# Attention weights transposed and multiplied for pairs of head groups; raw-row transposes between the down-projections

## The reference, cut to what matters

```python
x = x + xattn(layernorm(x), ctx)
    # q, k, v projections; scores = q k^T / sqrt(32)
    # out = softmax(scores) @ v            per head, 77 keys
    # h = relu(out @ W1 + b1); h @ W2 + b2
x = x + ffn(layernorm(x))
    # top1 = argmax(xn @ Wg.T); y = expert[top1](layernorm(xn))
```

## Time and profile before

| | us |
|---|---|
| median of three runs | 1548.53 (1547.26 to 1549.6) |
| the profiled execution | 1549.81 |
| its span, first to last instruction | 1548.0 |
| PE busy | 1503.9 |
| DVE busy | 1005.6 |
| ACT busy | 711.5 |
| POOL busy | 428.8 |

### The profile page before, as it was taken

The page is one execution under the profiler, slowest core; times in us unless marked ns, Lnnn a source line. Parts: engine busy times, 40 slices in busy tenths (PEclk is TensorE's granted clock), DMA queues, the critical chain, the costliest instruction groups (busy, mean ns, idle before and its releaser), DMA issues.

```text
span 1548.0 us, 24311 instructions
## 1 busy us (share of the span) xinstructions
PE 1503.9 (97%) x7988; PEld 1257.0 (81%) x7988; DVE 1005.6 (65%) x2489; ACT 711.5 (46%) x2015; POOL 428.8 (28%) x312
## 2 busy tenths in 40 slices
PE   7689999999999999999999999999999999999998
PEld 4578888888888787878788888888887878778986
DVE  5735656575857576666757585757574756559666
ACT  3534535354536363545445353535363635424554
POOL 2512212222222222212122112222222222117776
PEclk9799999999999999999999999999999999999999
DMA  9310110213020202131211201030202011458883
GB/s 231 113 55 28 31 53 7 76 26 108 13 89 28 89 28 75 36 97 42 75 42 40 78 15 61 16 110 1 82 1 83 1 55 55 171 172 282 243 238 120
DMA packets 76951, 122.71 MB, mean 79 GB/s; under 512 B 27990, under 2 KB 36455, under 8 KB 75806
## 3 DMA queue, kind: packets, MB, share of 16 engines
q1 hardware_dynamic: 66030, 87.47, 19.6%
q0 software_dynamic: 10800, 33.70, 5.7%
HBM read 76.24 MB, written 46.72 MB: 79 GB/s over the span
## 4 chain that ended last, share of the span: by engine, by line
PE 78%; DVE 14%; ACT 4%; issue 2%; DMA 1%; POOL 1%; POOLq 0%; DVEq 0%; SPq 0%; ACTq 0%
PE bank L1034 23%; PE bank L1056 20%; PE bank L896 11%; PE bank L920 5%; PE bank L1014 5%; DVE actH L1003 4%; PE bank L1457 4%; PE bank L1501 3%; ACT actH L997 2%; PE bank L1125 2%; PE bank L1440 2%; PE bank L864 2%; DVE E L941 1%; DVE mx L929 1%; DVE sm L968 1%
## 5 line engine op out<-in xcount | busy, mean ns | idle before, releaser
L1056 PE MATMUL bank<-w,actH 128*128 128x512 f32 x1536 | 371.1, 392 | 0.0
L1034 PE MATMUL bank<-actA,w 128*128 128x512 f32 x1536 | 366.8, 394 | 0.0
L1034 PEld LDWEIGHTS bank<-actA,w 128*128 128x128 f32 x1536 | 286.0, 188 | 62.3
L1056 PEld LDWEIGHTS bank<-w,actH 128*128 128x128 f32 x1536 | 283.1, 188 | 54.9
L979 POOL TENSOR_TENSOR E<-E,rc 128x1232 f32<-128x1232 f32 x64 | 145.0, 2266 | 464.6 <-DVE rc L974 464.6
L1041 ACT ACTIVATE actH<-bank,b 128x512 fp32r<-128x512 f32 x128 | 88.2, 689 | 228.8 <-PE bank L1034 228.8
L1046 DVE TENSOR_TENSOR actH<-bank,actH 128x512 fp32r<-128x512 f32 x128 | 87.8, 686 | 159.6 <-ACT bank L1042 159.6
L896 PE MATMUL bank<-actA,wq 128*128 128x512 f32 x768 | 182.0, 390 | 0.0
L952 ACT ACTIVATE E<-bank,mx 128x77 f32<-128x77 f32 x512 | 157.8, 364 | 42.1 <-DVE mx L929 42.1
L896 PEld LDWEIGHTS bank<-actA,wq 128*128 128x128 f32 x768 | 144.1, 188 | 30.4 <-issue 0.5
L1199 POOL DMA_INDIRECT region<-rows,pos x64 | 62.3, 974 | 373.2 <-DVE pos L1193 334.0
(11 more groups left out here) (166 smaller groups left out, 1970.2 us busy)
## 6 DMA issues: line engine op xcount, KB each, us to landing
rowB<-region SPq DMA_DIRECT2D x71, 258.0 KB, 3.8
xn<-in_x SPq DMA_DIRECT2D x64, 256.0 KB, 2.8
rows<-in_x SPq DMA_DIRECT2D x64, 256.0 KB, 3.2
e_raw<-in_E SPq DMA_DIRECT2D x16, 256.0 KB, 2.8
region<-padrow SPq DMA_DIRECT2D x9, 258.0 KB, 3.9
w_raw<-in_W SPq DMA_DIRECT2D x1, 2048.0 KB, 11.8
w_raw<-in_W SPq DMA_DIRECT2D x2, 1024.0 KB, 8.7
e_parts<-e_high SPq DMA_DIRECT2D x8, 256.0 KB, 2.0
```

The lines of the kernel that those rows point to most:

```text
L1034: mm = pe.matmul(p[:], w, a, start=k == 0 and j == 0, stop=k == KD - 1 and j == 2)
L1056: mm = pe.matmul(p[:], a, w, start=m == 0 and j == 0, stop=m == MF - 1 and j == 2)
```

## The change

- `PT` and `AV` run for two pairs of groups. A pair has 616 keys, cut into chunks of 128, 128, 128, 128 and 104. The third chunk holds keys of both groups. `AV` is three steps: i = 0 (chunks 0, 1), i = 1 (chunk 2), i = 2 (chunks 3, 4), each in a bank of its own. ACT copies the bank of i = 1 to `csb`, and DVE adds its last 32 rows to those of i = 0 and its first 32 to those of i = 2; only then both are copied and subtracted into `actA`.
- `TT` for tiles 0 to 2 stands in the score phase, behind the steps of groups 1 to 3; tile 3 and `L`, `LT` stand among `PT` and `AV`. The transposed rows go to `actA` instead of `actQ`, the logits to `csb`.
- The one-hot is a step of its own (`OH`) behind the subtraction of H2. The row statistics (`X2STAT`) begin to drip behind H0.
- H0 and H1 run their first three k-steps together, then the last one of each.
- `vbd` has pairs, and its loads are 24 pieces a batch instead of 12.

```diff
-CH = [103, 103, 102]
+CH = [128, 128, 128, 128, 104]
+CA, CC, CB = (0, 1), (2,), (3, 4)
...
         def attention_tail(b):
-            for c in range(NC):
-                step("PT", b, 0, c)
+            step("PT", b, 0, 0)
+            step("PT", b, 0, 1)
             step("SUM", b, KD - 1)
             if b:
-                step("X2STAT", b - 1)
-            for g in range(KD):
-                if g + 1 < KD:
-                    for c in range(NC):
-                        step("PT", b, g + 1, c)
-                if b and g == KD - 2:
-                    for s in range(SUB):
-                        step("TT", b - 1, s)
-                step("AV", b, g)
+                step("TT", b - 1, SUB - 1)
+            for c in range(2, NC):
+                step("PT", b, 0, c)
+            if b:
+                step("L", b - 1)
+            step("AV", b, 0, 0)
+            if b:
+                step("LT", b - 1)
+            step("AV", b, 0, 1)
+            step("PT", b, 1, 0)
+            step("AV", b, 0, 2)
+            for c in range(1, 4):
+                step("PT", b, 1, c)
+            step("AV", b, 1, 0)
+            step("PT", b, 1, 4)
+            step("AV", b, 1, 1)
+            step("AV", b, 1, 2)
...
+            if b:
+                step("X2STAT", b - 1)
             for m in range(MF):
...
-                if not (b and m == 2):
-                    step("HLO", b, m)
-                if b and m == 0:
-                    step("L", b - 1)
+                step("HLO", b, m)
...
                 if b and m == 2:
-                    step("LT", b - 1)
-                    step("HLO", b, m)
+                    step("OH", b - 1)
...
                     if g + 2 < KD:
                         step("Q", b + 1, g + 2)
+                    if g >= 1:
+                        step("TT", b, g - 1)
...
+        def dve_av(dve, b, pr, i):
+            n = NP * b + pr
+            if i == 0:
+                return
+            if i == 1:
+                dve.wait_ge(S["act_c"], n + 1)
+                dve_add(dve, b, pr, 0)
+                return
+            dve.wait_ge(S["pe_av"], 3 * n + 3)
+            dve_add(dve, b, pr, 2)
+            for h in (0, 2):
+                g = 2 * pr + h // 2
+                dve.wait_ge(S["act_o"], KD * b + g + 1)
+                dve.tensor_tensor(actA[:, 1, g, :], of("AV", b, pr, h)[:], f32(actA[:, 0, g, :]), ALU.subtract
+                                  ).then_inc(S["dve_o"], 1)
+
+        def dve_add(dve, b, pr, i):
+            p, r = of("AV", b, pr, i), PART[i]
+            dve.tensor_tensor(p[r, :], p[r, :], csb[r, :], ALU.add).then_inc(S["dve_c"], 1)
...
         def pe_h(pe, b, m):
+            if m == 0:
+                own_bank(pe, "H", b, 1)
+                for k in range(KD - 1):
+                    pe.wait_ge(S["dve_o"], KD * b + k + 1)
+                    h_products(pe, b, 0, k)
+                for k in range(KD - 1):
+                    h_products(pe, b, 1, k)
+                pe.wait_ge(S["dve_o"], KD * b + KD)
+            for k in range(KD - 1 if m < 2 else 0, KD):
+                mm = h_products(pe, b, m, k)
             mm.then_inc(S["pe_h"], 1)
```

More of the change, by code:

```diff
@@ L1004, in dve_pt, with pe_av @@
                               f32(actH[0:CH[c], 0, j % SLOTS, :]), ALU.subtract).then_inc(S["dve_pt"], 1)
-        def pe_av(pe, b, g):
-            p = own_bank(pe, "AV", b, g)
-            pe.wait_ge(ld_v, 16 * VLOADS * (b // BPB + 1))
-            for c in range(NC):
-                j = NC * g + c
-                pe.wait_ge(S["dve_pt"], NC * KD * b + j + 1)
-                for i, (v, w) in enumerate(split3([vbd[0:CH[c], h, g, c, :] for h in range(2)],
+        def pe_av(pe, b, pr, i):
+            p = own_bank(pe, "AV", b, pr, i)
+            if pr == 0 and i == 0:
+                pe.wait_ge(ld_v, 16 * VLOADS * (b // BPB + 1))
+            mine = (CA, CC, CB)[i]
+            for c in mine:
+                j = NC * pr + c
+                pe.wait_ge(S["dve_pt"], NC * NP * b + j + 1)
+                for t, (v, w) in enumerate(split3([vbd[0:CH[c], h, pr, c, :] for h in range(2)],
@@ L1013, in pe_av @@
                                                   [actH[0:CH[c], h, j % SLOTS, :] for h in range(2)])):
-                    mm = pe.matmul(p[:], v, w, start=c == 0 and i == 0, stop=c == NC - 1 and i == 2)
+                    mm = pe.matmul(p[:], v, w, start=c == mine[0] and t == 0, stop=c == mine[-1] and t == 2)
             mm.then_inc(S["pe_av"], 1)
-        def act_av(act, b, g):
-            act.wait_ge(S["pe_av"], KD * b + g + 1)
-            act.activation(actA[:, 0, g, :], of("AV", b, g)[:], ACT.Identity).then_inc(S["act_o"], 1)
@@ L1026, in pe_h @@
+        def dve_add(dve, b, pr, i):
+            p, r = of("AV", b, pr, i), PART[i]
+            dve.tensor_tensor(p[r, :], p[r, :], csb[r, :], ALU.add).then_inc(S["dve_c"], 1)
         def pe_h(pe, b, m):
-            p = own_bank(pe, "H", b, m)
+            if m != 1:
+                own_bank(pe, "H", b, m)
             if b == 0:
                 pe.wait_ge(S["pool_w1"], 2)
-            for k in range(KD):
-                pe.wait_ge(S["dve_o"], KD * b + k + 1)
-                for j, (w, a) in enumerate(split3([w1[:, h, k, P * m:P * m + P] for h in range(2)],
-                                                  [actA[:, h, k, :] for h in range(2)])):
-                    mm = pe.matmul(p[:], w, a, start=k == 0 and j == 0, stop=k == KD - 1 and j == 2)
@@ L1037, in act_h, with h_products @@
+        def h_products(pe, b, m, k):
+            p = of("H", b, m)
+            for j, (w, a) in enumerate(split3([w1[:, h, k, P * m:P * m + P] for h in range(2)],
+                                              [actA[:, h, k, :] for h in range(2)])):
+                mm = pe.matmul(p[:], w, a, start=k == 0 and j == 0, stop=k == KD - 1 and j == 2)
+            return mm
         def act_h(act, b, m):
@@ L1096, in x2T @@
         def x2T(b):
-            return x2T_last if b == NBLK - 1 else actQ
+            return x2T_last if b == NBLK - 1 else actA
         def pe_tt(pe, b, s):
```

116 lines of the change are left out of this document (66 added, 50 removed).

## The result

| | before | changed |
|---|---|---|
| median of the timed runs | 1547.89 us (1546.12 to 1549.6) | **1700.1 us** (1698.49 to 1703.81) |
| profiled execution | 1549.81 | 1703.81 |
| its span | 1548.0 | 1701.9 |
| PE busy | 1503.9 | 1525.6 |

A forecast was written before the change was run, and what follows sets the result against it. PE, busy 97% of the span, bounds the kernel. To 1549.8 us the walk added 15 x (3.65 + 0.2 + 1.6) + 8 x 4.6 - 1 = 118, removed work deducted, giving 1668; the clock's 32 made 1700, range 1625 to 1745.

The forecast's parts named there:

- Removed work: PE's 6 matmuls and 8 transposes fewer a block: 2.2 us a block, 35 us in all, if nothing waits.
- A: PE's wait at the second chunk transpose for DVE's addition of the last row tile: 2.4 us, 15 times.
- B: PE's wait at the gate product for DVE's subtraction of raw tile 3: 3.3 us, 15 times.
- C: PE's waits at AV of the second pair: 1.0 us in two parts, 0.2 more at the last chunk, 15 blocks.
- E: PE's wait at the e_acc product after H1, in eight blocks preparing expert weights: 4.6 us, bounds 3.4 and 5.2.
- F: PE's wait for the one-hot after H3, at its first matmul: 1.6 us in 15 blocks, bounds 0.5 and 2.1.
- `vbd` loads: Doubled loads on SP's queue in three blocks delay xn loads: 0, at worst 4 us in the block preparing no weights.
- The clock: Low PE clock after idle waits: 12 us behind E, 20 behind A and B in half of the blocks; 32 together.
- rival 1: PE's clock stays up despite the waits, so the time is 1668; chance 0.25.
- rival 2: The clock falls in every tail and at every E wait, costing 3 us each: about 1725; chance 0.15.
- rival 3: Only the waits in H are real; ACT and DVE have room to hide the tail: 1580; chance 0.1.
- rival 4: Faster: DVE runs far enough ahead that PE's removed work is the whole effect, 1515; chance 0.03.

The follow-up runs named there:

- e11: e7 with the vbd loads moved behind the loads of the next block's rows and of the raw expert weights; 1522.8 us (0.9832).
- e3: Changed kernel with raw-row tile 1 transposed after the scores of group 3 instead of behind those of group 2; 1667.5 us (1.0749).
- e4: Changed kernel with the sum of the fourth group behind raw tile 3 and the last chunk of pair 0; 1663.6 us (1.0731).
- e1: Changed kernel with the e_acc sums issued on DVE ahead of H0's subtraction; 1658.0 us (1.069).
- e2: Changed kernel with the rank products behind H4 instead of H3; 1688.65 us (1.0894).
- e5: Changed kernel with the four edits of e1, e2, e3 and e4 together; 1569.6 us (1.0136).
- e6: Changed kernel with extra transposes, results overwritten, on PE during its waits at the gate product (24) and the e_acc product (38); 1679.7 us (1.0848).
- e7: Changed kernel with e1's and e2's edits, raw tiles, sum, gate product and pair 1 transposes reordered, H0 and H1 sharing two k-steps first; 1540.8 us (0.9954).
- e12: Changed kernel with the edits of e1 and e2 together; 1648.8 us (1.0635).
- e9: Changed kernel with only the vbd loads moved behind the token loads of the next block; 1704.6 us (1.0989).
- e10: Changed kernel with only the pairs of groups, merge and vbd kept; raw rows, gate, one-hot, statistics and H0, H1 as before the change; 1595.8 us (1.0296).

## Why the prediction was right, step by step

- **Removed work**, 2.2 us a block: 2.6 by e11. The twelve transposes of 128 columns take 1.47, those of 103 took 1.48, so width cost nothing. My other reason was weak: the 158 ns of the earlier trace rows is a mean over two shapes, 172 for 103 columns and 132 for 102, so it says little about width. The changed kernel's weight loads take 149 for 128 columns and 146 for 104. The rule of the Trainium skill that I had set against it ("TensorE: Matmul & The Clock Gate", "Step-by-step: what each phase is for") does not show in the time here.
- **A**, 2.4: 2.02 idle, 2.21 from start to start (from the start of the transposes ahead of it to the next start, less 0.103 a transpose; the idle time of a trace begins after the last transpose has drained). Cause shown by e3.
- **B**, 3.3: 2.83, or 3.06 from start to start. Cause shown by e4: a later sum takes 1.6 off it.
- **C**, 1.2 with its second part: 0.76. H0's wait of 0.2: its 24 matmuls take 5.95 for 5.5.
- **E**, 4.6: 4.12. From H0's start to the product it is 10.07, less 5.52 of matmuls 4.55, where the walk had 4.8 with H0's wait. Cause shown by e1.
- **F**, 1.6 (its own terms add up to 1.5): 1.3. e2 took it away.
- **`vbd` loads**, 0 with 4 as the worst: 2.7 in the block that prepares no weights (91.9 against 89.2). Inside the bound of 4, and so small only because E covers the loads in the other two blocks (e1).
- **The walk as a whole.** A block that prepares no weights takes 89.17 for 82.0, less 1.56 of clock 5.6; the walk had 5.45. The others take 95.4 for 82.48, less some 3.0 of clock 9.9; the walk had 10.05. Of the 152 us of the loss some 118 are left without the clock, and the walk had 118.
- **The clock**, 32: 34.2, but not for the reasons given. I had E at 12: eight falls of 2.7, less 9.6 because F would shrink. It is 16.3: a fall costs 2.0 on average there, and F does not shrink (1.3 in each of 14 blocks). I had the tail fall in half of the blocks at 2.7 each, 20; it falls in all 15, is paid in 12, and costs 1.5 there, 17.9. The Trainium skill's rule on bursts and waits (the same page, "HAM oscillation — how this bites in real kernels") holds for the changed kernel in that every tail falls; the tails of e5, with waits of 1.1 us and less, have no fall. Priced at 2.7 each it gave 20 us too much, since a part of the low clock falls into a wait.

So rival 1 (the clock stays up) is refuted by e6 and by the granted clock. Rival 2 is refuted in its price though not in its count, rival 3 (the tail is hidden) and rival 4 by the waits A and B. What made the forecast hold was the walk through three queues; from start to start its waits A, B and E are 5 to 10% too long. That the clock's share came out right was luck: in the tail a count too low met a price too high, and behind E a price too high met a deduction that did not come.

The walk was right for the kernel as it stood. Its prices were worth less for what a removed wait gives back: eight of the twelve expectations were off by 8 us or more. In e5, e7 and e12 the `vbd` loads lost the cover of a wait, in e4 and e12 the fall of the clock went or moved, in e6 the fill overran the waits that it was to fill, e2 stays open in part, e9 moved loads that were still covered, and for e10 I had not walked the queues again.

## What to carry to other kernels

When a step goes into another place of a written order, walk the other engines too: a small copy behind a batch of exponentials, with DVE's next work behind its subtraction, cost here about as much (33 us, e3) as all that PE saved (35). Take each new wait away in turn and all together, and look at which blocks stay long, for the largest waits hide the loads and chains behind them. A change that saves PE work and measures slower may hold a gain: as many instructions, reordered with the loads last in the queue, went from 1.0987 to 0.9832.

## What was not expected of the hardware

- The clock fell after an idle time of 2.0 us with 20 transposes behind it (909.40 to 914.70, granted 0.68), not only behind the 3.4 and 4.6 us of the start-up. In the tails of e5, with waits of 1.1 us and less, it did not fall. Where in such a stretch it falls changes from block to block of one run.
- What a fall costs depends on what follows: nothing in the 3 tails where the low clock ended ahead of a wait, 1.5 on average in the other 12, 2.0 behind E.
- Keeping PE busy through its waits, with 24 transposes a block and 38 more in eight of them, gave 20 us though their results are not used (e6).
